# Attention and mixture of experts on one core: parts of q and k stored one by one, maxima by half groups, padding rows skipped

## The reference

```python
mod = (_silu(L0_c) @ L0_wmod).reshape(L0_c.shape[0], 6, 1, -1)
sa, ca, ga, sb, cb, gb = (mod[:, 0], mod[:, 1], mod[:, 2], mod[:, 3], mod[:, 4], mod[:, 5])
ga = (2 * (ga >= 0) - 1) * jnp.maximum(jnp.abs(ga), 0.25)
gb = (2 * (gb >= 0) - 1) * jnp.maximum(jnp.abs(gb), 0.25)
h = _layernorm(x, axis=-1) * (1 + ca) + sa
x = x + ga * _L0_attn_ref(h, L0_attn_Wq, L0_attn_Wk, L0_attn_Wv, L0_attn_Wo)
h = _layernorm(x, axis=-1) * (1 + cb) + sb
x = x + gb * _L0_ffn_ref(h, ...)
...
scores = jnp.einsum('bhqd,bhkd->bhqk', q, k) / math.sqrt(hd)
attn = jax.nn.softmax(scores, axis=-1)
...
_, idx = jax.lax.top_k(logits, K)
h = jax.nn.silu(jnp.einsum('nd,edh->enh', xt, we1) + be1[:, None, :])
eo = jnp.einsum('enh,ehd->end', h, we2) + be2[:, None, :]
y = xt + jnp.einsum('ne,end->nd', w, eo)
```

## Time and profile before

| | us |
|---|---|
| median of 3 runs (lowest to highest) | 1045.59 (1044.89 to 1048.23) |
| profiled execution: own time | 1044.19 |
| profiled execution: span from the first to the last instruction | 1042.4 |
| busy: PE, DVE, ACT, POOL | 876.1, 781.8, 739.6, 362.6 |
| block attend starts | 87.4 |
| first exponential | 148.7 |
| last exponential ends | 828.8 |
| first load of block mix | 838.2 |
| last tile's sum on DVE | 1021.5 |

### The profile page before, as it was taken

How to read it: one execution, slowest core, us unless ns; L and a number is a source line. 1 busy time by engine, 2 the same in 40 slices (tenths; PEclk the granted TensorE clock), 3 DMA queues, 4 the chain that set the end, 5 groups by cost and what they waited for, 6 DMA issues and landing times. The chain is left out here.

```text
span 1042.4 us, 17839 instructions
## 1 busy us (share of the span) xinstructions
PE 876.1 (84%) x5934; PEld 349.5 (34%) x5934; DVE 781.8 (75%) x1042; ACT 739.6 (71%) x1620; POOL 362.6 (35%) x662
## 2 busy tenths in 40 slices
PE   3653469999999989999999999998988779988981
PEld 1330012222222222222222222222222178887971
DVE  6656979999998897999898899989861026632375
ACT  3541028888888888788888888888888756555651
POOL 4532000000000254044027206223523537678873
PEclk7866559999999999999999999999999989999996
DMA  4364030404403000072000000100000112122453
GB/s 131 121 254 176 25 138 1 168 9 162 158 13 138 32 2 31 3 212 73 2 31 3 31 27 29 50 2 31 3 1 9 34 49 63 55 65 78 142 139 98
DMA packets 60186, 72.69 MB, mean 70 GB/s; under 512 B 9569, under 2 KB 41825, under 8 KB 60097
## 3 DMA queue, kind: packets, MB, share of 16 engines
q1 hardware_dynamic: 55264, 61.82, 18.3%
q0 software_dynamic: 4544, 9.35, 2.6%
q10 hardware_dynamic: 288, 0.40, 0.1%
HBM read 30.08 MB, written 41.06 MB: 68 GB/s over the span
## 5 line engine op out<-in xcount | busy, mean ns | idle before, releaser
L870 DVE TENSOR_REDUCE half_max<-ps_max 128x2 f32<-128x1024 f32 x512 | 601.2, 1218 | 67.4 <-PE ps_max L688 58.2
L803 ACT ACTIVATE probs<-ps_scores 128x512 f32<-128x512 f32 x1024 | 539.1, 604 | 94.2 <-PE ps_scores L709 92.6
L722 PE MATMUL ps_ctx<-probs,v_grp 128*32 128x512 f32 x2048 | 275.1, 609 | 0.7 <-ACT probs L803 0.7
L709 PE MATMUL ps_scores<-q_set,k_set 51*128 51x512 bf16 x1024 | 258.5, 389 | 15.9 <-ACT probs L803 12.1
L688 PE MATMUL ps_max<-k_set,q_set 48*128 48x512 bf16 x1024 | 193.8, 404 | 57.3 <-DVE half_max L870 41.9
L709 PEld LDWEIGHTS ps_scores<-q_set,k_set 51*128 51x128 bf16 x1024 | 68.8, 93 | 326.9 <-ACT probs L803 303.8
L1522 ACT ACTIVATE hid<-ps_up,w_tile 128x128 f32<-128x128 f32 x312 | 89.0, 368 | 55.2 <-PE ps_up L1688 55.1
L1487 POOL DMA_INDIRECT y_rows<-y,y_to x78 | 93.0, 1193 | 38.5 <-DVE y L1559 22.7
L688 PEld LDWEIGHTS ps_max<-k_set,q_set 48*128 48x128 bf16 x1024 | 50.5, 95 | 164.9 <-DVE half_max L870 148.6
L1688 PE MATMUL ps_up<-slots_t,w_tile 128*128 128x128 f32 x624 | 85.4, 281 | 6.9 <-DVE w_tile L1553 6.6
L1559 DVE TENSOR_TENSOR y<-ps_down,w_tile 128x128 f32<-128x128 f32 x78 | 22.7, 291 | 89.8 <-PE ps_down L1698 78.7
(11 more groups left out here) (201 smaller groups left out, 640.9 us busy)
## 6 DMA issues: line engine op xcount, KB each, us to landing
slots<-zero_rows SPq DMA_DIRECT2D x43, 387.0 KB, 6.2
q_terms<-parts SPq DMA_DIRECT2D x24, 256.0 KB, 2.7
k_terms<-parts SPq DMA_DIRECT2D x24, 256.0 KB, 3.2
q_set<-q_terms SPq DMA_DIRECT2D x32, 192.0 KB
k_set<-k_terms SPq DMA_DIRECT2D x32, 192.0 KB
slots_in<-slots SPq DMA_DIRECT2D x78, 64.5 KB, 1.9
rows<-y_rows SPq DMA_DIRECT2D x16, 256.0 KB, 4.8
w_all<-in_we SPq DMA_DIRECT2D x1, 2048.0 KB
```

The source lines that it names most:

```text
L709: pe.matmul(bank[:], k_set[g % SETS][operand, u, tile * P:(tile + 1) * P], q_set[g % SETS][operand, u, c * BANK:(c + 1) * BANK], start=Tru ...
L722: ins = pe.matmul(ps_ctx[32 * head:32 * head + 32, :], v_grp[g % 2][:, tile, head, :], probs[:, s % RING, head, :], start=tile == 0, stop= ...
L803: act.activation(probs[:, s % RING, place, :], ps_scores[n % BANKS_S][:], ACT.Exp, scale=float(HD) ** -0.5).then_inc(slot_taken, 1)
L870: dve.reduce_max(half_max[g % 2][:, c, 2 * u:2 * u + 2, tile], ps_max[n % 2][:].rearrange("p (r n) -> p r n", r=2), axis=AX.X).then_inc(ma ...
```

## The change

The following is changed:

- prepare: `store_parts` goes part by part, each part with semaphores of its own (`part_ready`, `part_stored`); the cast into part 0 of the next batch waits for part 0's stores alone. SP loads all three sets in prepare, right behind batch 0's stores (before: the first set behind batch 1's, the others in attend). POOL, DVE and PE take batch 0's norm and modulation ahead of batch 1's; the arithmetic on the gates moves on DVE from ahead of batch 0's rotary product to behind its parts.
- attend: maxima go by half groups of 16 units: 16 units stand ahead of the first join, 16 more ahead of step 0, and there are 32 joins, splits, transposes and sets of four row DMAs (half as wide) where there were 16. DVE's wait for the tables moves behind the 32 units.
- mix: slots without a token hold the row number `NOWHERE`, beyond the bound, and the scatter leaves them out. `address` is gone: the scatter reads the integer row from the slot itself. `QRING` is 12, and a slot buffer is free when its scatter has landed. DVE loads the next expert's number behind the copy of the weights.

```diff
-QRING = 8
+QRING = 12
+NOWHERE = 1 << 24
+Y_ROWS = 2 * B * S
...
 def store_parts(sp, k, b):
-    for qk, name in enumerate(("q_terms", "k_terms")):
-        terms = k[name].rearrange("t (b g) r f u n -> t b (g r f u) n", b=B)
-        sp.wait_ge(k["parts_ready"], 2 * b + qk + 1)
-        for n, term in enumerate(TERMS):
-            sp.dma_start(terms[n, b], k["parts"][qk][:, term[qk], :]).then_inc(k["parts_stored"], 16)
+    for part in range(3):
+        for qk, name in enumerate(("q_terms", "k_terms")):
+            terms = k[name].rearrange("t (b g) r f u n -> t b (g r f u) n", b=B)
+            sp.wait_ge(k["part_ready"][part], 2 * b + qk + 1)
+            for n, term in enumerate(TERMS):
+                if term[qk] == part:
+                    sp.dma_start(terms[n, b], k["parts"][qk][:, part, :]).then_inc(k["part_stored"][part], 16)
...
-            norm_scale(0)
-            norm_scale(1)
-            modulate(0)
-            modulate(1)
-            for b in range(2, B):
+            for b in range(B):
                 norm_scale(b)
                 modulate(b)
...
-                if b:
-                    act.wait_ge(parts_stored, 16 * 2 * len(TERMS) * b)
-                for qk in range(2):
-                    act.wait_ge(rot_ready, 2 * b + qk + 1)
-                    act.copy(parts[qk][:, 0, :], rot[qk][:]).then_inc(part0_ready, 1)
...
+                for part, (made, whole) in enumerate(((rot_ready, rot), (rest_ready, rest))):
+                    if b:
+                        act.wait_ge(part_stored[part], stored_by(b, part))
+                    for qk in range(2):
+                        act.wait_ge(made, 2 * b + qk + 1)
+                        act.copy(parts[qk][:, part, :], whole[qk][:]).then_inc(part_ready[part], 1)
...
 def negated_in(s):
-    g = (s + 5) // STEPS
-    return g if (s + 5) % STEPS == 0 and 0 < g < NG else None
+    h = (s + 5) // NT
+    return h if (s + 5) % NT == 0 and 0 < h < HALVES else None
...
 def units(s):
-    first = UNITS + LEAD + 2 * s
+    first = HALF_UNITS + LEAD + 2 * s
...
-            for n in range(UNITS):
+            for n in range(HALF_UNITS + TURN_LEAD):
                 max_scores(n)
             turn_negated(0)
-            for n in range(UNITS, UNITS + LEAD):
+            for n in range(HALF_UNITS + TURN_LEAD, HALF_UNITS + LEAD):
                 max_scores(n)
...
             def load(n):
                 if n >= QRING:
-                    sp.wait_ge(y_to_ready, n - QRING + 1)
-                    sp.wait_ge(slots_t_ready, n - QRING + 1)
+                    sp.wait_ge(y_out[(n - QRING) % YRING], 16 * ((n - QRING) // YRING + 1))
...
-            def address(n):
-                pool.wait_ge(slots_loaded[n % QRING], 16 * (n // QRING + 1))
-                if n >= YRING:
-                    pool.wait_ge(y_out[n % YRING], 16 * (n // YRING))
-                pool.tensor_scalar(y_to[n % YRING][:], slots_in[n % QRING][:, D:], float(n % YRING), None,
-                                   ALU.max).then_inc(y_to_ready, 1)
             def send(n):
-                pool.wait_ge(y_to_ready, n + 1)
+                pool.wait_ge(slots_loaded[n % QRING], 16 * (n // QRING + 1))
                 pool.wait_ge(y_ready, n + 1)
-                pool.indirect_dma_start(k["y_rows"], bass.IndirectOffsetOnAxis(y_to[n % YRING][:, 0:1], axis=0),
-                                        y[n % YRING][:], None).then_inc(y_out[n % YRING], 16)
+                to = slots_in[n % QRING][:].bitcast(I32)[:, D:]
+                pool.indirect_dma_start(k["y_rows"], bass.IndirectOffsetOnAxis(to, axis=0),
+                                        y[n % YRING][:], None, bounds_check=Y_ROWS - 1,
+                                        oob_is_err=False).then_inc(y_out[n % YRING], 16)
...
+            e = expert(WRING - 1)
             for n in range(ALL_TILES):
                 later = n + WRING - 1
-                if later < ALL_TILES:
-                    e = expert(later)
                 add_bias(n)
                 if later < ALL_TILES:
                     copy_w(later, e)
+                if later + 1 < ALL_TILES:
+                    e = expert(later + 1)
```

More of the change, by code:

```diff
@@ L49 @@
 LEAD = 16
+HALVES = 2 * NG
+HT = NT // 2
+HALF_UNITS = GH * HT
 UNITS = GH * NT
+TURN_LEAD = 4
 ALL_UNITS = NG * UNITS
@@ L144, in build @@
             k["parts"] = [operands.enter_context(nc.sbuf_tensor(f"parts{i}", [P, 3, S], BF16)) for i in range(2)]
-            for name in ("parts_ready", "parts_stored"):
-                k[name] = operands.enter_context(nc.semaphore(name))
+            for name in ("part_ready", "part_stored"):
+                k[name] = [operands.enter_context(nc.semaphore(f"{name}{i}")) for i in range(3)]
             prepare(nc, t, k)
@@ L244, in _ @@
                 sp.dma_start(dst[:], src).then_inc(later_consts_in, 16)
-            for b in range(2):
+            store_parts(sp, k, 0)
+            for part in range(3):
+                sp.wait_ge(part_stored[part], stored_by(1, part))
+            for g in range(SETS):
+                load_set(sp, k, g)
+            for b in range(1, B):
                 store_parts(sp, k, b)
-            load_set(sp, k, 0)
-            store_parts(sp, k, 2)
             sp.wait_ge(later_consts_in, 16 * len(later_loads))
@@ L468, in beside @@
     found = []
-    if (g := negated_in(s)) is not None:
-        found.append(("negated", g))
+    if (h := negated_in(s)) is not None:
+        found.append(("negated", h))
     if (chunk := turned_in(s)) is not None:
@@ L503, in split_in @@
     last = units(s)[1]
-    return last // UNITS if last is not None and last % UNITS == UNITS - 1 else None
+    return last // HALF_UNITS if last is not None and last % HALF_UNITS == HALF_UNITS - 1 else None
 def attend(nc, t, k):
@@ L577, in load_weights @@
                                  t["we2"][e].rearrange("(c p) d -> p c d", p=P)).then_inc(k["weights_in"], 16)
-            for g in range(1, SETS):
-                load_set(sp, k, g)
-            store_parts(sp, k, B - 1)
             negated_rows(0)
-            sp.wait_ge(k["parts_stored"], 16 * 2 * len(TERMS) * B)
+            for part in range(3):
+                sp.wait_ge(k["part_stored"][part], stored_by(B, part))
             per_group = 9
+            negated_rows(1)
             for g in range(1, NG):
@@ L588, in _ @@
                     load_weights()
-                negated_rows(g)
-                if g + SETS - 1 < NG:
+                for c in range(2):
+                    negated_rows(2 * g + c)
+                    if c or g + SETS - 1 >= NG:
+                        continue
                     sp.wait_ge(set_used, g)
@@ L671, in _ @@
             split_max(0)
+            split_max(1)
             for s in range(ALL_STEPS):
@@ L703, in scores @@
                 head, g, c, tile = place, s // STEPS, s // NT % 2, s % NT
-                if s % STEPS == 0 and place == 0:
-                    pe.wait_ge(rows_in[g % SETS], 16 * GH * (g // SETS + 1))
+                if s % NT == 0 and place == 0:
+                    pe.wait_ge(rows_in[g % SETS], 16 * GH * (2 * (g // SETS) + c + 1))
                 bank = bank_of((s, place))
@@ L893, in step @@
                     invert_sums(chunk)
-                if (g := split_in(s)) is not None:
-                    join_halves(g)
+                if (h := split_in(s)) is not None:
+                    join_halves(h)
             def route_piece(s, place):
@@ L917, in _ @@
             route = route_on_dve(dve, k, r)
-            dve.wait_ge(r.tables_ready, r.TABLES)
-            for n in range(UNITS):
+            for n in range(HALF_UNITS):
                 take_max(n)
             join_halves(0)
-            for n in range(UNITS, UNITS + LEAD):
+            for n in range(HALF_UNITS, HALF_UNITS + LEAD):
                 take_max(n)
+            join_halves(1)
+            dve.wait_ge(r.tables_ready, r.TABLES)
             for s in range(ALL_STEPS):
@@ L1389, in mix @@
         y = [sb(f"y{i}", [P, D]) for i in range(YRING)]
-        y_to = [sb(f"y_to{i}", [P, 1], I32) for i in range(YRING)]
         rows = [[sb(f"rows{i}_{n}", [P, NT, D]) for n in range(2)] for i in range(EARLY)]
```

135 lines of the change are left out of this document (72 added, 63 removed).

## The result

The changed kernel takes 1003.67 us (median of 4 executions, 1001.83 to 1007.23), the kernel before took 1045.84 beside it; the ratio is 0.9598, interval 0.9566 to 0.9629. The forecast was 1004. The profiled execution took 1003.83, its span is 1002.0 for 1042.4.

| stretch | before | after | measured | forecast |
|---|---|---|---|---|
| start to PE's first unit in attend | 87.44 | 78.37 | -9.1 | -14.9 |
| that to DVE's first unit | 5.43 | 0.65 | -4.8 | -4.8 |
| first unit to first exponential | 55.84 | 35.36 | -20.5 | -20.3 |
| first exponential to the end of the last | 680.13 | 687.59 | +7.5 | +12.2 |
| that to the end of the kernel (mix) | 213.5 | 200.0 | -13.5 | -14 |

The account below looks back on a forecast made before the run. No engine was taken to bound the whole; each stretch had its own bound. Terms -14.9 - 4.8 - 20.3 + 7.8 + 2.4 + 2 - 14 = -41.8 took 1045.6 to 1003.8, say 1004 us, range 987 to 1021.

Parts of the forecast that it names:

- Prepare, -14.9: Prepare: earlier batch 0 and storing part by part start attend at 72.5 instead of 87.4 us; bounds -11 to -18.
- Rival 2: Prepare: batch 1's stores behind twelve loads on SP's queue delay batch 2's casts; gains 7 for 15, 1012 us; chance 0.13.
- Tables, -4.8: Start of attend: without waiting for POOL's tables, DVE's first unit runs 0.65 behind the block's start, for 5.43; 4.8 us saved.
- half the lead, -20.3: Attend: half groups shorten first unit to first exponential from 55.84 to 35.5 us; 20.3 saved.
- More turned maxima, +7.8: Attend's steps: 31 turned maxima for 15, so 16 more at 0.49 us each; 7.8 us added.
- units beside the last routing, +2.4: Attend, steps 232 to 239: these now have units beside the last routing; 2.4 us added.
- Weights, +2: Attend: issuing the experts' weights between two half groups' rows makes them land later; 2 us added, bounds 0 and +5.
- Mix, -14: Mix: 6 us from the stall, 2 from earlier combining rows, 6 from the expert's number; bounds 0 and -24.
- 1: Mix: DVE and POOL take turns and POOL stays the bound; gains 2 for 14, 1016 us; chance 0.17.
- 4: Mix: the bound makes a send dear and POOL sets the pace; slower, 1066 us at sends of 2.3; chance 0.05.
- 5: Attend: row DMAs late at each half, 16 stalls of 1.5 eat the half groups' 20 us; 1026 us; chance 0.02.
- 3: More gained: fewer rows shorten POOL's sends, mix's stall goes whole, prepare gains 18; 988 us; chance 0.13.

Follow-up runs that it names:

- tables_ahead: The changed kernel, but DVE waits for POOL's tables ahead of its first unit again; 1007.08 us, ratio 0.9636.
- whole_groups: The changed kernel, but attend's maxima go by whole groups again instead of half groups; 1017.11 us, ratio 0.9733.
- number_ahead: The changed kernel, but DVE loads the expert's number ahead of each sum again; 1009.36 us, ratio 0.9655.
- stores_whole: The changed kernel, but SP stores q's six copies once all its parts are there, then k's, not part by part; 1019.57 us, ratio 0.975.
- sets_behind_b1: The changed kernel, but sets 1 and 2 are loaded behind batch 1's stores instead of ahead of them; 1000.44 us, ratio 0.9574.
- rings_12_16: sets_late_lead14 with 12 buffers of y for 8 and 16 of slots for 12; 1001.0 us, ratio 0.9547.
- sets_late_lead14: sets_in_attend with 30 units instead of 32 ahead of step 0 (LEAD = 14); 998.04 us, ratio 0.954.
- address_back: The changed kernel, but POOL makes an address per tile again for the scatter, padding rows still left out; 1012.77 us, ratio 0.969.
- rows_written: address_back, but slots without a token write to eight spare rows again and the scatter has no bound; 1018.52 us, ratio 0.9743.
- sets_in_attend: The changed kernel, but sets 1 and 2 are loaded at the start of attend instead of in prepare; 1000.1 us, ratio 0.9571.

## Why the prediction was right, point by point

**What bounds.** That no engine bounds the whole, and that each stretch has to be read by itself, held: the table's stretches moved by their own causes, and undoing one edit moved its stretch alone, to within some 1 us (tables_ahead the first unit, whole_groups lead and steps, number_ahead the tiles).

**Prepare, -14.9.** The mechanism was right (stores_whole: 16.0), the size was not: 9.1, outside the term's own bounds of 11 to 18. The step that failed is "its stores, from 43.7 on, keep up with that". They were issued in time, 44.29 to 54.04, but six sixteenths of each landed late, behind the loads' data, the last at 62.4. Rival 2 had named the place, at 7 for 15, and its sign came, ACT's wait of 5.69 for a store; it put it down to SP's queue, where sets_behind_b1 shows the transfers. With sets 1 and 2 loaded in attend it starts at 74.05. The 1.5 left of the forecast's 72.5 is the stretch from batch 2's first cast to its copy of v, 6.8 (52.43 to 59.26) where the sum has 4.7: the second cast waits for its rotary product (53.84), and DVE's two differences, which run beside POOL's modulation, take 4.55 where batch 3's take 2.42.

**Tables, -4.8, and half the lead, -20.3.** Both to 0.2 us, in the trace and when undone (4.78, 20.46).

**More turned maxima, +7.8, and units beside the last routing, +2.4.** The second is the 2.58 of group 14, with a turned maximum in it that cannot be told apart (the earlier trace rows give 2.50). The first was mis-sized: 0.49 is right in plain groups, but I multiplied it by 16, where groups 5, 6, 9, 10 and 13 paid 0.15 or less. In all it came to 5.1, the 7.5 less 2.4. A price read from steps without routing on DVE holds for such steps.

**Weights, +2.** Nothing: groups 7 and 8 take 41.11 and 43.29, only the 0.49 and 0.46 of every such group above before. It was within the bounds of 0 to 5, at their lower end.

**Mix, -14.** 13.5, and between first and last sum 13.8. By stretch in the two traces, tiles 37 to 45 are 5.4 shorter (forecast 6), the sum behind the first combining piece comes 2.0 sooner (forecast 2), and the rest, tiles beside DVE's long pieces above all, is 6.4 (forecast 6). Undone one by one, the parts cost 6.3 (number) and 7.9 (address; forecast 6 and 2). Two effects were missed and stand against each other. The padding rows are worth some 5 us with POOL's addresses back, forecast 0: "transfers wait for nobody here" was wrong, since rows and buffers wait for landings. And the slot buffers' new rule, forecast "a few tenths", costs 16 more with 8 buffers than with 12; how much 12 leave was not measured. So that the whole came out right may in part again be a balance.

**The rivals.** 1 fell with number_ahead, 4 and 5 with the sends of 0.99 and the steps at each half, which show no wait for rows. 3 was right in one point, that fewer rows help, though through landings.

## What to carry to other kernels

When a load is moved ahead of stores, look at how many DMA engines its shape lets it use, not only at its place in the queue: twelve loads that kept little over a third of the engines busy had the stores behind them land up to 11.7 us after their issue, for 3.7 with four loads ahead. A price per event from a quiet stretch need not hold in a busy one; count the events by stretch before multiplying. And the slack of a produced value is not its distance in steps but what stands ahead of the producer on its queue: two units decided between 998 and 1036.

## What the runs showed of the hardware that I had not expected

The granted clock can fall in one execution of a program and stay up in another. The profiled execution of rings_12_16, one of the three long ones, in windows (columns as above):

```profile
760.00:770.00 10.00, 8.73 (x53) 2.56 (x49) 3.47 (x9) 8.65 (x19) 5.35 (x22) 0.98 0.01 2
770.00:780.00 10.00, 9.47 (x36) 1.18 (x35) 4.12 (x13) 4.89 (x11) 7.87 (x8) 0.50 0.15 48
790.00:800.00 10.00, 9.21 (x36) 1.08 (x28) 0.00 (x0) 5.24 (x12) 7.59 (x9) 0.50 0.14 46
```

In the last steps of attend, which have no maxima any more, the clock goes from the upper level (2.4 GHz) to the lower (0.50, 1.2 GHz) and stays there to the end of the block; a step then takes 3.69 for 2.39, and eleven of them make the 14 us. PE had been busy 8.73 of 10 us before the fall. The changed kernel's trace has 1.00 in the same steps, with PE busy 8.0 to 9.4 of 10 us from 760 to 790. One of the six executions of sets_late_lead14 took 1010.7 as well: the mean granted clock is 0.925 to 0.927 in these four and 0.945 to 0.949 in the other eight. The edit of the rings touches nothing ahead of mix, so the rings need not be the cause. What decides it is open.

A scatter that leaves out rows by a bound takes POOL no longer than one without: 1.04 each where POOL makes the addresses (address_back and rows_written), and 0.98 to 0.99 in the changed kernel, which reads them from the slot.

DVE's differences of two SBUF tensors take longer beside POOL's modulation, which has two SBUF inputs as well: in sets_in_attend 4.55 for two in batch 2, and 2.42 in batch 3, where POOL is idle.
